# Routed experts on one core: the third tile of the next group is turned right behind the first two, into another bank of PSUM

## The reference

```
q, k, v = split(x, 3, axis=1)                        # 125 tokens' rows each, 16,000 tokens in all
h   = softmax over channels of (q k^T, scaled) applied to v
h   = h + attention(layernorm(h))                    # 8 heads, 2 key-value heads, softcap 50
xf  = layernorm(h)                                   # 16,000 rows of 512
scores = softmax(xf @ gate_w);  sel = top 2 of 8 experts of (scores + bias)
out = (silu(xf @ sw1) * (xf @ sw3)) @ sw2            # shared expert
for each token and each of its 2 experts e:
    r = xf[token] * score
    out[token] += (silu(r @ w1[e]) * (r @ w3[e])) @ w2[e]     # 512 -> 448 -> 512
h = h + out
```

## Time and profile before

| | |
|---|---|
| median of three runs | 5922.34 us (5916.81 to 5924.61) |
| profiled execution, its own time | 5922.86 us |
| profiled execution, its span | 5921.1 us |
| mean granted TensorE clock | 0.991 |
| PE matmul busy | 5784.0 us, 98% |
| PE weight load busy | 5009.4 us, 85% |
| DVE busy | 4450.0 us, 75% |
| ACT busy | 3084.8 us, 52% |
| POOL busy | 2101.8 us, 35% |

### The profile page before, as it was taken

How to read it: one execution, slowest core, us unless ns; L and a number is a source line. 1 busy time by engine, 2 the same in 40 slices (tenths; PEclk the granted TensorE clock), 3 DMA queues, 4 the chain that set the end, 5 groups by cost and what they waited for, 6 DMA issues and landing times. The chain is left out here.

```text
span 5921.1 us, 109291 instructions
## 1 busy us (share of the span) xinstructions
PE 5784.0 (98%) x32259; PEld 5009.4 (85%) x32259; DVE 4450.0 (75%) x10104; ACT 3084.8 (52%) x5748; POOL 2101.8 (35%) x1711
## 2 busy tenths in 40 slices
PE   5999999999999999999999997899999999999999
PEld 4888888888888888888888886899999999999998
DVE  4888888888888888888888886666666766666665
ACT  3555555555555555555555553555555555555554
POOL 1333333333333333333333332333434444444343
PEclk8999999999999999999999999999999999999999
DMA  2111111111111111111111111777777777777762
GB/s 73 47 50 44 44 49 46 43 47 49 43 45 50 44 44 49 46 43 47 49 43 45 50 44 25 190 188 187 184 189 182 182 187 188 183 189 182 184 167 79
DMA packets 363663, 565.45 MB, mean 95 GB/s; under 512 B 92898, under 2 KB 187106, under 8 KB 363492
## 3 DMA queue, kind: packets, MB, share of 16 engines
q1 hardware_dynamic: 294276, 433.22, 24.2%
q0 software_dynamic: 69344, 131.70, 11.3%
HBM read 438.14 MB, written 138.42 MB: 97 GB/s over the span
## 5 line engine op out<-in xcount | busy, mean ns | idle before, releaser
L1438 POOL DMA_INDIRECT out_dram<-res,goal x273 | 560.8, 2054 | 1070.4 <-DMA entries<-routed_entries 480.8
L930 POOL TENSOR_SCALAR ve<-ag 125x1 f32<-125x1 f32 x256 | 56.1, 219 | 1618.3 <-DVE ag L755 942.2
L639 ACT ACTIVATE e<-ps,negmax 128x512 f32<-128x512 f32 x512 | 348.6, 685 | 513.5 <-PE ps L449 409.8
L1188 PE MATMUL ps<-rT_hi,up_hi 128*128 128x384 f32 x2548 | 552.3, 338 | 1.6 <-DVE rT_lo L1348 1.6
L1188 PE MATMUL ps<-rT_lo,up_hi 128*128 128x384 f32 x2548 | 552.1, 338 | 0.0
L1188 PE MATMUL ps<-rT_hi,up_lo 128*128 128x384 f32 x2548 | 552.0, 338 | 0.0
L1278 ACT ACTIVATE uT_hi<-egb 128x384 fp32r<-128x384 f32 x364 | 191.4, 526 | 572.3 <-DVE egb L1367 561.5
L1188 PEld LDWEIGHTS ps<-rT_hi,up_hi 128*128 128x128 f32 x2548 | 457.8, 188 | 9.8 <-issue 2.0
L1188 PEld LDWEIGHTS ps<-rT_lo,up_hi 128*128 128x128 f32 x2548 | 456.3, 188 | 0.0
L1188 PEld LDWEIGHTS ps<-rT_hi,up_lo 128*128 128x128 f32 x2548 | 456.2, 188 | 0.0
L942 POOL TENSOR_TENSOR qk_low<-X,qk_high 125x1024 fp32r<-125x1024 f32 x128 | 306.3, 2393 | 345.7 <-ACT qk_high L626 345.7
(11 more groups left out here) (220 smaller groups left out, 15549.2 us busy)
## 6 DMA issues: line engine op xcount, KB each, us to landing
raw<-in_L_ffn_w SPq DMA_DIRECT2D x182, 768.0 KB, 5.1
X<-in_x SPq DMA_DIRECT2D x128, 750.0 KB
raw<-in_L_ffn_w SPq DMA_DIRECT2D x91, 896.0 KB
raw<-in_L_ffn_w SPq DMA_DIRECT2D x273, 128.0 KB, 5.0
normed_rows<-y SPq DMA_DIRECT2D x128, 250.0 KB
out_dram<-h SPq DMA_DIRECT2D x128, 250.0 KB
rows<-normed_rows,entries POOLq DMA_INDIRECT x273
out_dram<-res,goal POOLq DMA_INDIRECT x273
```

Source lines behind the costliest of these rows:

```text
L639: nc.scalar.activation(e[:, i, :], ps[:, (i + 1) % 2, :], ACT.Exp, bias=negmax[:, i:i + 1], accum_out=total[:, i:i + 1]).then_inc(e_sb.sem, 1)
L1188: ins = nc.tensor.matmul(ps[:, bank, 0:GROUP], w[a][:, k, col:col + P], rT[b][:, k, :], start=(k == 0 and i == 0), stop=(k == KC - 1 and i ...
L1438: nc.gpsimd.indirect_dma_start(out, bass.IndirectOffsetOnAxis(ap=goal[group[1] % 2][:, i:i + 1], axis=0), res[i][:], None, bounds_check=la ...
```

## The change

Tile 2 is turned right behind tiles 0 and 1, ahead of the lower products, and goes to bank 5. For that it waits on `gb_sb` of block 1 of the group at hand: the gate that read bank 5 last. All three turns wait on `rT_lo` of the same tile of the group before. ScalarE and VectorE read the turned tile 2 from bank 5.

```diff
@@ -1057,6 +1057,7 @@
             LAST_IN_BANK = (1, 3, 2)
+            TURN_BANK = (0, 1, 5)
             HALF = HID + TAIL
@@ -1174,9 +1175,11 @@
                         pe.wait_ge(scaled.sem, scaled.at(t))
-                        pe.wait_ge(rT_lo.sem, rT_lo.at(back(t, LAST_IN_BANK[i])))
+                        pe.wait_ge(rT_lo.sem, rT_lo.at(back(t, T)))
+                        if TURN_BANK[i] >= 2:
+                            pe.wait_ge(gb_sb.sem, gb_sb.at(block_of(back(group, 1), 1)))
                         for k in range(KC):
-                            last = nc.tensor.transpose(ps[:, i % 2, k * P:(k + 1) * P],
+                            last = nc.tensor.transpose(ps[:, TURN_BANK[i], k * P:(k + 1) * P],
                                                        rows[i][:, k * P:(k + 1) * P], ident[:])
@@ -1233,12 +1236,11 @@
                         if left:
                             turn_rows(after, 0)
                             turn_rows(after, 1)
+                            turn_rows(after, 2)
                         down_full(group, 0)
                         down_full(group, 1)
                         down_tail(group, 0)
                         down_tail(group, 1)
-                        if left:
-                            turn_rows(after, 2)
                         down_full(group, 2)
                         down_tail(group, 2)
@@ -1263,7 +1265,7 @@  rows_hi, and the same at 1347 in rows_lo
-                        nc.scalar.activation(rT[0][:, :, i * P:(i + 1) * P], ps[:, i % 2, :].rearrange(
+                        nc.scalar.activation(rT[0][:, :, i * P:(i + 1) * P], ps[:, TURN_BANK[i], :].rearrange(
```

More of the change, by code:

```diff
@@ L1347, in rows_lo @@
                         part = slice(i * P, (i + 1) * P)
-                        nc.vector.tensor_tensor(rT[1][:, :, part], ps[:, i % 2, :].rearrange(
+                        nc.vector.tensor_tensor(rT[1][:, :, part], ps[:, TURN_BANK[i], :].rearrange(
                             "p (k c) -> p k c", k=KC), rT[0][:, :, part].bitcast(F32), ALU.subtract).then_inc(rT_lo.sem, 1)
```

## The result

The changed kernel takes 5960.16 us (median of six, 5956.93 to 5963.71) against 5920.34 us for the kernel before (5916.81 to 5924.61). The ratio is 1.0067, with a 95% interval of 1.0054 to 1.008: slower by 0.67%. The forecast was 5960.5 us.

What follows compares the result with a forecast made beforehand. TensorE was taken to set the pace at 24.00 us a group. The turn's + 39.2 us less 1.1 us at the start made + 38.1 us, so 5960.5 us; own range 5953 to 5972, with the runs' spread 5951 to 5972.

Steps and rivals of the forecast that it cites:

- The turn ahead of the lower products costs 0.435 us in each of 90 groups: Tile 2's four transposes behind the first eight: nothing covers them, + 39.2 us in all.
- Taken from its old place it gives nothing: Behind the tails, the turn lay inside tile 2's wait for the copy of tile 0's result; removing it gives 0.
- The third wait among the transposes costs 0: New wait on `gb_sb` of block 1: always met, taken as 0, upper bound 0.1 us or 9 us in all.
- Earlier rows at ScalarE bring nothing: ScalarE's 1.92 us idle before `rows_hi` of tile 2 goes, but nobody waits for its earlier high parts: no gain.
- The start gains 1.1 us: At the routed stage's start, tile 2's own bank lets its low part end 1.4 us earlier, worth 0.8 to 1.4 us.
- The wait of the weight loads grows to 0.65 us, 57 us in all: At tile 2's `down_full`, weight loads wait for the copy of tile 0's result, 0.21 us a group before.
- Rival 1: The wait before tile 2's `down_full` comes from leaving the transposes, not from the copy, and goes: 5899 us; 3%.
- Rival 2: TensorE's clock falls in the longer run of transposes and the wait: 80 us more, about 6040 us; 3%.
- Rival 3: The turn is hidden ahead of the lower products too, another chain setting the group's 24.00 us: 5921 us; 4%.
- The total: Whole kernel: + 39.2 - 1.1 = + 38.1 us, forecast 5960.5 us, 0.64% slower.
- the middle groups' copy answers 0.1 us later than that of the first and last: VectorE's copy starts 0.53 us after tile 0's last tail matmul against 0.43 in the last group; waits compare with registers.

Runs made afterwards that it cites:

- short_run: The changed kernel with one transpose instead of four for tile 2 in 90 groups: 5928.45 us, 1.0013 of the kernel before.
- short_old: The kernel before with one transpose instead of four for tile 2, at its old place, in 90 groups: 5921.79 us, ratio 1.0002.
- own_bank_old: The kernel before with tile 2's lower product in bank 4 instead of bank 6, its turn still behind the tails: 5900.32 us, ratio 0.9961.
- bank_only: The kernel before with tile 2 turned into bank 5 and the change's waits, but at its old place behind the tails: 5918.69 us, ratio 0.9998.
- tails_old: The kernel before with the tails of tiles 0 and 1 each right behind its own main part: 5926.05 us, ratio 1.0007.

## Why the prediction was right

- *The turn ahead of the lower products costs 0.435 us in each of 90 groups.* Right: 0.428 us by the group's length, 38.5 us in all against 39.2; short_run gives 0.110 us for a transpose, the prediction had 0.109.
- *Taken from its old place it gives nothing.* Right: 0.80 us between the same two starts against 0.81, and in short_old 0.005 us for three transposes. That this is the wait for bank 6 is shown by own_bank_old, where the wait and 0.23 us of each group go.
- *The third wait among the transposes costs 0.* Right within about 0.01 us of a group. In bank_only it leaves the wait for the copy as it was. In the run, 0.110 us for each transpose taken off 24.427 (four) or 24.096 (one) leaves 23.986 us, and the group of before has 23.999.
- *Earlier rows at ScalarE bring nothing.* Right: its idle time is gone and no wait elsewhere went with it. GpSimd's gather did not come earlier either.
- *The start gains 1.1 us.* In these two executions it gained 1.48 us up to the first upper product and 1.45 us up to group 0's first turn (3740.44 - 3713.09 = 27.35 against 3739.27 - 3710.47 = 28.80), just above the upper end, 1.4. Whether the clock's rise follows the products stays open. Here the first twelve upper products run at the lower level in both, for 3.98 us (3723.75 to 3727.73) and 3.97 us (3722.61 to 3726.58). But in bank_only, which starts as early, the first sixteen do (3720.14 to 3725.39), and its first turn comes after 28.17 us. Over all traces this distance is 28.66 to 29.59 us in the seven kernels with the old start, 29.03 on average, and 27.09 to 28.25 us in the five with the new one, 27.65 on average. So the gain is 1.4 us on average, and one pair of executions could not have told it from 0.8.
- *The wait of the weight loads grows to 0.65 us, 57 us in all.* Wrong: 0.84 us, 75.7 us in all, though the time lost is as forecast. The load before the wait was one of the transposes and ended late; now it is that of the tail's last matmul, which is made one matmul ahead. The idle time of the loads grew by 0.63 us and the group by 0.43. The distance from start to start, from which the sum was made, does not have this fault.
- *Rival 1, the wait goes with the turn:* excluded by the result and by short_old. *Rival 2, the clock falls:* it is 1.00 with twelve transposes in 1.3 us and the longer wait. The two rules of the Trainium skill (TensorE: Matmul & The Clock Gate, Part 4: PE-mode transpose, and A second HAM failure mode) do not show themselves at this size; had the clock fallen by them, the time would have been longer than measured. *Rival 3, hidden at the new place too:* excluded, the time is 0.67% longer and over 0.5% even at the interval's lower end.
- *The total.* That it is met within 0.4 us is in part luck. The kernel before measured 2.0 us less than the 5922.34 us the forecast started from (5920.34), and the difference between the medians is 39.8 us against 38.1 forecast and against 38.5 - 1.4 = 37.1 from the parts as measured. The rest is of the size by which the first stage varies. The range's ends also don't follow from its terms: their plain sum would be 5954 to 5976 us, not 5953 to 5972. The measured time lies well inside both.
- That the middle groups' copy answers 0.1 us later than that of the first and last because its waits compare with registers was argued only. No run here tests it.

## What to carry to other kernels

In this kernel work inside a wait was free, and the same work beside it was not. Before moving a step, compare the distance between the starts around it with and without the step (here the first, the middle and the last group had both cases in one trace). The cover has a depth, 0.67 us here. It can be filled (two turns), made needless (another bank for what waits, or the release brought forward), and what is then the best order of the rest is a new question: the order that lost 40 us was as good as the old one or better once the wait was gone.

## What the runs showed of the hardware that I had not expected

After a wait TensorE loses about 0.1 us more than the wait. In tails_old the second matmul starts 0.34 us behind the first and not 0.23, and the first one's weight load begins with it and not ahead of it. The changed kernel has the same behind its wait for the copy: the next pass starts 0.80 us after 4504.67, where a pass otherwise takes 0.70. The earlier trace rows already has the same 0.80 us (4513.69 to 4514.49). In the prediction it is inside the 0.68 us of rival 1, and is not named as a price of the wait.
